# GAT walks of a graph kernel: the source rows of one turn fetched by ScalarE, one copy for each row, at addresses from registers

## What is computed

```python
h = (x @ W).reshape(num_nodes, H, C)                      # H = 4 heads of C = 32
e = leaky_relu(alpha_src[src] + alpha_dst[dst], 0.2)
m = segment_max(e, dst); e = exp(e - m[dst])
out = segment_sum(h[src] * (e / den[dst])[:, :, None], dst)
```

## Time and profile before

| | |
|---|---|
| runs | 6567.3, 6568.11, 6572.21 us; median 6568.11 |
| span of the profiled execution | 6570.3 us, from the first to the last instruction |
| DVE busy | 4654.6 us, 71% of the span |
| POOL busy | 4293.2 us, 65% |
| ACT busy | 1375.2 us, 21% |
| first to last turn of a GAT walk | some 975 us, twice |

### The profile page before, as it was taken

How to read it: one execution, slowest core, us unless ns; L and a number is a source line. 1 busy time by engine, 2 the same in 40 slices (tenths; PEclk the granted TensorE clock), 3 DMA queues, 4 the chain that set the end, 5 groups by cost and what they waited for, 6 DMA issues and landing times. The chain is left out here.

```text
span 6570.3 us, 37158 instructions
## 1 busy us (share of the span) xinstructions
PE 1251.3 (19%) x8049; PEld 1094.3 (17%) x8049; DVE 4654.6 (71%) x9455; ACT 1375.2 (21%) x3580; POOL 4293.2 (65%) x4445
## 2 busy tenths in 40 slices
PE   7100000145555534332000000810000010000000
PEld 6100000135544433322000000610000010000000
DVE  7788888799999969987888887744444444444445
ACT  0122222220111114431000000622222211222223
POOL 0777777667777760027777775367777767777775
PEclk9555555555555555556555555955555555555555
DMA  9666666433443437754666664123333323333332
GB/s 391 199 218 202 202 199 204 130 106 131 132 136 133 133 115 292 295 184 153 220 219 218 225 218 158 30 85 109 113 111 109 115 74 90 112 113 109 113 111 82
DMA packets 338944, 1032.97 MB, mean 157 GB/s; under 512 B 100325, under 2 KB 163137, under 8 KB 331294
## 3 DMA queue, kind: packets, MB, share of 16 engines
q0 software_dynamic: 166752, 401.68, 21.4%
q1 hardware_dynamic: 116642, 342.34, 14.8%
q10 hardware_dynamic: 55324, 286.57, 12.1%
HBM read 602.97 MB, written 427.39 MB: 157 GB/s over the span
## 5 line engine op out<-in xcount | busy, mean ns | idle before, releaser
L725 POOL DMA_INDIRECT rows<-table,idx x3136 | 2987.4, 953 | 985.0 <-issue 973.1
L644 POOL DMA_INDIRECT by_src<-ebuf,place x784 | 767.4, 979 | 275.0 <-issue 238.3
L1296 DVE SCALAR_TENSOR_TENSOR psA<-psA,cont,dstf 128x128 f32<-128x128 f32 (+1 forms) x2349 | 836.6, 356 | 48.0 <-ACT ebuf L1025 27.2
L1285 DVE TENSOR_TENSOR sc<-rows,ebuf 128x56 f32<-128x56 f32 x112 | 28.2, 252 | 1023.9 <-DMA rows<-table,idx 1023.9
L958 PE MATMUL psA<-dstf,ones 128*128 128x512 f32 x10 | 9.9, 1113 | 3055.3 <-DVE dstf L2223 3055.3
L1296 DVE SCALAR_TENSOR_TENSOR sums<-sums,cont,psA 128x128 f32<-128x128 f32 (+1 forms) x1512 | 518.9, 343 | 30.3 <-ACT psA L1221 29.0
L958 PEld LDWEIGHTS psA<-dstf,ones 128*128 128x128 f32 x10 | 2.7, 317 | 3056.9 <-issue 3056.9
L823 PE MATMUL psA<-attr,sums 128*128 128x49 f32 x1568 | 406.1, 403 | 470.8 <-DVE attr L1475 470.8
L2104 DVE TENSOR_TENSOR_SCAN psA<-rows,psA 128x1980 f32<-128x1980 f32 x112 | 480.0, 4286 | 3.9
L823 PEld LDWEIGHTS psA<-attr,sums 128*128 128x128 f32 x1568 | 397.0, 326 | 476.9 <-DVE attr L1475 476.9
L1227 ACT ACTIVATE psA<-df 128x60 f32<-128x60 f32 (+1 forms) x168 | 40.4, 241 | 1714.2 <-DVE df L1285 1714.2
(11 more groups left out here) (350 smaller groups left out, 5533.6 us busy)
## 6 DMA issues: line engine op xcount, KB each, us to landing
dstf<-spread_wide SPq DMA_DIRECT2D x168, 924.0 KB
states<-sums ACTq DMA_DIRECT2D x150, 952.0 KB, 4.0
rows<-by_src SPq DMA_DIRECT2D x55, 1035.0 KB, 5.1
states<-sums ACTq DMA_DIRECT2D x56, 1008.0 KB, 5.7
spread_wide<-sums SPq DMA_DIRECT2D x56, 924.0 KB, 24.7
states<-sums ACTq DMA_DIRECT2D x56, 903.0 KB, 7.4
rows<-table,idx POOLq DMA_INDIRECT x3136
msg<-low_rows SPq DMA_DIRECT2D x56, 448.0 KB, 3.7
```

The costliest lines, as they stand in the source:

```text
L644: pool.indirect_dma_start(by_src[:, :], bass.IndirectOffsetOnAxis(ap=place[:, s, j:j + 1], axis=0), payload[:, s, j, :], None).then_inc(so ...
L725: pool.indirect_dma_start(rows[:, at:at + GW[ph]], None, table[ph][:, :], bass.IndirectOffsetOnAxis(ap=idx[:, s, j:j + 1], axis=0)).then_i ...
L1285: return dve.tensor_tensor(o_, a_, b_, op)
L1296: return dve.scalar_tensor_tensor(o_, a_, s_, b_, op0, op1)
```

## The change

Each GAT walk leaves turn 54 out of POOL's gathers. ACT fetches the 1792 rows of that turn during turns 0 to 53: behind the save of each turn it takes two or three partitions, loads the 14 node numbers of each into registers, and issues one DMA for each row, from the table at an address computed from the register to the tile `msg`, which lies idle in these phases. DVE reads turn 54 from `msg` and waits for `side_landed`. The other 55 turns go on alternating between the two slots. In all walks the tile `idx` is gone with its copies and waits: POOL's gathers take their offsets from `src` itself.

```diff
+SIDE = {3: 54, 4: 54}
...
+        def row_slot(ph, g):
+
+            side = SIDE.get(ph, NG)
+            return None if g == side else (g - int(g > side)) % 2
...
+        def free_at(ph, g):
+
+            s = row_slot(ph, g)
+            users = [k for k in range(g) if row_slot(ph, k) == s]
+            return 2 + TURN[ph] * NG + (users[-1] + 1 if users else 0)
...
-                            pool.wait_ge(idx_staged, g + (1 + TURN[ph] * (NG + 2)))
-                            pool.wait_ge(rows_used, g + (1 + TURN[ph] * NG))
...
-                                                        bass.IndirectOffsetOnAxis(ap=idx[:, s, j:j + 1], axis=0)).then_inc(rows_landed[s], 16)
+                    for g in range(NG):
+                        s = row_slot(ph, g)
+                        if s is None:
+                            continue
+                        pool.wait_ge(rows_used, free_at(ph, g))
...
+                                                    bass.IndirectOffsetOnAxis(ap=src[:, g * B + j:g * B + j + 1], axis=0)).then_inc(rows_landed[s], 16)
...
+                def side_rows(parts):
+
+                    w, at = GW[ph], SIDE[ph] * B
+                    for p in parts:
+                        act.load(numbers_of, src[p:p + 1, at:at + B])
+                        for j in range(B):
+                            node = act.snap(numbers_of[j])
+                            act.dma_start(msg[p:p + 1, j * w:(j + 1) * w], table[ph][bass.ds(node, 1), :]).then_inc(side_landed[ph], 16)
...
-                        act.wait_ge(rows_used, g + (3 + TURN[ph] * NG))
-                        act.activation(idx[:, s, :], src[:, bass.ds((g + 2) * B, B)], ACT.Copy).then_inc(idx_staged, 1)
...
+                        if g < SIDE.get(ph, 0):
+                            side_rows(range(g * P // SIDE[ph], (g + 1) * P // SIDE[ph]))
...
-                        dve.wait_ge(rows_landed[s], it * (16 * B) + (16 * B + TURN[ph] * IT * 16 * B))
+                        if row_slot(ph, g) is None:
+                            dve.wait_ge(side_landed[ph], 16 * B * P)
+                        else:
+                            dve.wait_ge(rows_landed[row_slot(ph, g)], landed_at(ph, g))
```

More of the change, by code:

```diff
@@ L97, in build @@
         aux = sb("aux", [P, NB, 136])
-        src = sb("src", [P, CH + 2 * B], I32)
+        src = sb("src", [P, CH], I32)
         cont = sb("cont", [P, CH])
@@ L360, in build @@
         dve_step = sem("dve_step")
-        idx_staged = sem("idx_staged")
+        side_landed = {p: sem(f"side_landed{p}") for p in SIDE}
         rows_landed = [sem(f"rows_landed{s}") for s in range(2)]
@@ L439, in scattered_at, with slot_turns, landed_at, turn_rows @@
             return 16 * KB * (ph * turns + g // ZS + 1)
+        def row_slot(ph, g):
+            side = SIDE.get(ph, NG)
+            return None if g == side else (g - int(g > side)) % 2
+        def slot_turns(ph, s, g=NG):
+            return sum(row_slot(ph, k) == s for k in range(g))
+        def landed_at(ph, g):
+            s = row_slot(ph, g)
+            before = sum(slot_turns(q, s) for q in TURN if q < ph)
+            return 16 * B * (before + slot_turns(ph, s, g) + 1)
+        def free_at(ph, g):
+            s = row_slot(ph, g)
+            users = [k for k in range(g) if row_slot(ph, k) == s]
+            return 2 + TURN[ph] * NG + (users[-1] + 1 if users else 0)
+        def turn_rows(ph, g):
+            s = row_slot(ph, g)
+            tile = msg[:, 0:B * GW[ph]] if s is None else rows[:, s * B * GW[ph]:(s + 1) * B * GW[ph]]
+            return tile.rearrange("p (b w) -> p b w", b=B)
         FIRST_LOADS = 6
@@ L715, in _ @@
                         pool.wait_ge(tab_saved, 16 * KG * TURN[ph])
-                    for it in range(IT):
-                        for s in range(2):
-                            g = it * 2 + s
-                            pool.wait_ge(idx_staged, g + (1 + TURN[ph] * (NG + 2)))
-                            pool.wait_ge(rows_used, g + (1 + TURN[ph] * NG))
[L721 to L725, removed]
-                                                        bass.IndirectOffsetOnAxis(ap=idx[:, s, j:j + 1], axis=0)).then_inc(rows_landed[s], 16)
+                    pool.wait_ge(src_in, 48)
+                    if ph:
+                        pool.wait_ge(n_kept, (2 if ph == 2 else 3) * KG)
+                    for g in range(NG):
+                        s = row_slot(ph, g)
+                        if s is None:
+                            continue
+                        pool.wait_ge(rows_used, free_at(ph, g))
+                        if g == 1 and ph < 3:
+                            spreads_landed()
+                        for j in range(B):
+                            at = (s * B + j) * GW[ph]
+                            pool.indirect_dma_start(rows[:, at:at + GW[ph]], None, table[ph][:, :],
+                                                    bass.IndirectOffsetOnAxis(ap=src[:, g * B + j:g * B + j + 1], axis=0)).then_inc(rows_landed[s], 16)
                     for s in range(2):
@@ L1058, in sorted_pass @@
                                   ssums[g % 3]).then_inc(pass_saved[g % 3], 16)
+            numbers_of = [act.alloc_register(f"side_row{j}") for j in range(B)]
             low_digits()
@@ L1197, in _ @@
                     sorted_pass()
[L1198 to L1201, removed]
                 def chain_gates(g):
@@ L1210, in _ @@
                     chain_gates(0)
+                    act.wait_ge(src_in, 48)
+                    act.wait_ge(tab_saved, 16 * KG * TURN[ph])
                 for it in range(IT if ph != 1 else 0):
@@ L2109, in turn @@
                         ahead = not (last and s)
-                        G3 = rows[:, s * B * GW[ph]:(s + 1) * B * GW[ph]].rearrange("p (b w) -> p b w", b=B)
+                        G3 = turn_rows(ph, g)
                         S3 = sums[:, s * B * W:(s + 1) * B * W].rearrange("p (b w) -> p b w", b=B)
```

1 line of the change is left out of this document (removed).

## The result

The changed kernel takes **7739.98 us** (median of 4 runs, 7738.24 to 7742.4) against 6569.12 us before (4 runs, 6567.3 to 6572.21). The ratio is 1.1781, with a 95% interval from 1.1764 to 1.1797. The forecast was 7245 us: the direction and the way were right, and the price was 495 us too small.

A forecast was written before the change was run, and what follows sets the result against it. POOL's gathers bound the GAT walks before; afterwards ACT alone would, at 9.02 + S a turn. Copies 11.6 plus loads 3.3 gave S = 14.9 us, +676 us on 6570, so 7245 us; range 6590 to 7900 us.

The forecast's parts named there:

- What bounds the walk before: GAT walks: POOL is never held up, its 14 gathers make a turn of 17.56 us; one turn less saves 35.1 us in two.
- Nothing for `idx`: Removing the idx copies and waits counts as nothing, at most 9.5 us; offsets read from src cost nothing.
- The change goes into the pause between save and exponential, and it doesn't fit: ACT's sequencer in a GAT turn: 14.9 us of added work against a pause of 8.54 us, over by 6.4 us.
- The law, 108 S - 933 us: Change of both GAT walks together once ACT alone sets the turn at 9.02 + S; no change at S = 8.64 us.
- S: ACT sequencer time added per GAT turn: 11.6 us for 33.2 copies plus 3.3 us for 2.37 loads, 14.9 us.
- tail of 21.3 us: End of a GAT walk, turns 54 and 55: 3.3 us for last rows and scores plus two chains of 9.02 us.
- The issue, 0.25 us a copy: ACT's sequencer issuing one row's DMA: 0.25 us, ends 0.22 and 0.33 us, taken from SP's one-partition loads and ACT's save.
- The register instruction with its gap, 0.06 us: ACT's sequencer, one register instruction for each copy, gap included: 0.06 us, between nothing and 0.20 us.
- The load, 1.4 us: ACT loading 14 node numbers into registers: 1.4 us, between 0.16 and 1.9 us, 2.37 times a turn.
- The 7600 us: Alternative sum at the skill's 200 ns a register: a load takes 2.8 us, S 18.2 us, the kernel about 7600 us.
- faster kernel: Rival: ACT's added work fits the 8.54 us pause, POOL stays the bound, two turns are saved: 6533 us; 12%.
- backed-up queue: Rival: 33 copies in a row clog ACT's queue, S = 28.5 us, +2145 us, about 8710 us; 5%.

The follow-up runs named there:

- turn_left_out: Changed kernel without loads and copies; in each GAT walk nobody fetches turn 54, DVE works on slot 1's earlier rows: 6540.54 us, ratio 0.9953 to the kernel before.
- no_side: Changed kernel with all 56 turns gathered by POOL again, idx still removed and offsets from src: 6572.49 us against 6571.77 before, ratio 1.0002.
- fixed_rows_2: Changed kernel with ACT copying fixed table rows, no register loads or address computations, wrong rows for turn 54: 6877.45 us against 6575.3 before, ratio 1.0459.
- gates_behind: Changed kernel with ACT's gates of the next turn moved behind the row copies instead of ahead of the save: 7916.79 us, ratio 1.2042 to the kernel before.
- one_part_in_scan: Changed kernel with one of each turn's two or three partitions fetched ahead of ACT's wait for the scan: 6995.35 us, ratio 1.064 to the kernel before.
- sp_fetches: Changed kernel with SP making all row loads and copies from the start of the walk, ACT none: 6654.03 us, ratio 1.0127 to the kernel before.
- one_copy_a_load: Changed kernel with all loads but only the first of 14 rows copied, turn 54 on slot 1; slower chip: 7465.29 us, ratio 0.9899 to the kernel before.
- fixed_rows: Changed kernel with ACT copying fixed table rows, no register loads or address computations; on the slower chip: 7690.6 us, ratio 1.0198 to the kernel before there.
- sp_and_act: Changed kernel with SP fetching 112 partitions, ACT 16, one behind each third save; on the slower chip: 8514.26 us, ratio 1.1323 to the kernel before there.
- sp_and_act_2: Changed kernel with SP fetching 112 partitions and ACT 16, one behind each third save, on another chip: 6541.95 us against 6575.3 before, ratio 0.995.

## Why the prediction was right, and where its sizes failed

- **What bounds the walk before**, POOL's 14 gathers a turn: right. Leaving one turn out saved 15.6 us a walk where 17.56 were counted, because the last two steps need 10.2 us each for the chain and the scores (turn_left_out).
- **Nothing for `idx`**: right (no_side, 1.0002).
- **The change goes into the pause between save and exponential, and it doesn't fit**: right. ACT's exponential waits for "issue" alone, 18.2 us a turn (582.2 / 32), and POOL for DVE.
- **The law, 108 S - 933 us**: right at two whole kernels: S = 19.36 gives +1158 us, measured +1166 between the spans; S = 11.4 gives +298, measured +302. The first holds by construction if S is read from the walk; here it is added up from the sequencer's instructions. Its tail of 21.3 us came out by luck in part: turn 54's exponential starts 2.5 us behind the last copy instead of 3.3, and turn 55's 1.1 us behind the save instead of at once.
- **The issue, 0.25 us a copy**: 0.234 us measured. 33.2 x 0.016 = 0.5 us too much.
- **The register instruction with its gap, 0.06 us**: this term failed. A copy has two of them, 0.044 and 0.029 us, and three gaps of 0.03 us instead of the two that were counted. The part of a copy that isn't the issue is 0.163 us against 0.10: 33.2 x 0.063 = 2.1 us too little. The order of the changed kernel's instructions shows one ISA row for each copy; the MOVE is only in the trace.
- **The first copy behind a load**: not foreseen, 0.6 us a turn.
- **The load, 1.4 us**: right for 148 of 256 (1.4 to 1.6), and wrong by 1.8 us for the 108 behind a save. 5.3 us a turn against 3.3 is 2.0 us too little.

The terms add up: 14.9 - 0.5 + 2.1 + 0.6 + 2.0 = 19.1 us, and the 0.31 us gaps make it 19.36. Each microsecond of S is 108 us of time, so the 4.5 us missing are some 480 of the 495 us.

Two ends in the prediction's cases don't follow from its own law: S = 8.8 us gives +17 us and not 13, and S = 23 us gives 8120 us and not 8050. Neither moves the forecast.

The Trainium skill ("Runtime: NRT & Kernel Launch", Instruction fetch mechanics) states about 200 ns for each register of a load. The same page of the Trainium skill (The ~15µs preamble/postamble breakdown) speaks of register loads from HBM, while these read from `src` in SBUF. Here 14 registers took 1.4 to 1.6 us where nothing disturbed, 0.11 us each; the measurement decides. The 7600 us that the prediction worked out by that rule came nearer to the result than its own sum, but for another reason: a load of 2.8 us everywhere stands in for long ones behind saves and for the dearer copies.

Of the rivals, the faster kernel came true only where SP took seven eighths of the rows. The backed-up queue didn't appear: in the changed kernel the longest issue is 0.502 us, and in fixed_rows_2 the long ones (up to 1.181 us) are the third and fourth behind a save and not those behind many copies.

## What to carry to other kernels

An engine that is busy for a fifth of the time may have no long pause where the work has to go: measure the pause between its last duty of one turn and its first of the next, and count every sequencer instruction of the moved work in it, the hidden ones and the gaps too. For a one-row copy at a register address that was 0.397 us, not the 0.234 us of its issue, and it was paid in full, 33 times a turn. The same work can be worth doing on a queue with nothing behind it that others wait for: SP and ACT together kept the turn's whole 31 us, as SP's share ended (893 us) before the walk did (949 us).

## What the runs showed of the hardware

**A register load takes twice as long while the save moves, and copies are held up too.** In the changed kernel, gates_behind and one_part_in_scan, each load that starts less than 1 us behind the end of a save's issue takes 3.0 to 3.5 us and ends 3.0 to 3.6 us behind it, 108 of 108 in each; all the others take 1.4 to 1.6 us. The loads of SP in sp_fetches, on another queue, do the same: 11 that begin within 1 us behind ACT's save take 2.80 to 3.48 us, 5 from 1 to 2 us behind it 1.98 to 2.49 us, and another 20 that begin up to 0.7 us before the end of the save's issue take 1.86 to 3.53 us. The rest take 1.3 to 1.7 us. One-row copies are held up in the same stretch: the third and fourth behind a save in fixed_rows_2, and in sp_fetches 83 issues of SP over 0.7 us, all within 2 us of the end of ACT's save. (Worked out by setting each start against the end of the last or next save's issue.) The save lands some 4.3 us after its issue:

```profile
L1285 ACTq DMA_DIRECT2D states<-sums x224: 326/330/366, 254.4 to 7633.4; - x112
...
DMA to landing us min/median/max: 3.6/4.3/8.2
```

In the changed kernel's DMA records the 128 packets of 7616 bytes of such a save run from 0.9 to 3.4 us behind the end of its issue, in the median. That is the stretch in which the loads and copies are slow. So the cause isn't the queue, the gates or the row copies, and it goes with the save's 952 KB. What they contend for, no run shows, and no run changes the save's size.

**An issue right behind another takes longer.** In fixed_rows_2, from 3 us behind a save on, a copy issued 0.03 us behind another takes 0.27 us (2913 copies), and one issued 0.3 us behind another takes 0.22 us (24 of 24). With a register address, where the two extra instructions lie between two issues, it takes 0.234 us. So the 0.274 us of fixed_rows_2 goes with the short distance and not with the fixed address. The first copy behind a load takes 0.47 us on ACT, also where only one follows (0.468 us in one_copy_a_load), but 0.26 us on SP.

**Sequencer time can differ from chip to chip.** On the slower chip the kernel before took 7522 us instead of 6570, fixed_rows took 12% longer than on another chip and sp_and_act 30%. In sp_and_act most of the stalls are some 0.7 us long: SP has 1117 pauses of 0.6 to 0.75 us and ACT 526, where sp_and_act_2, the same kernel on another chip, has 0 and 19. Why, no run shows.
